# Feature biases of two graph attention layers: from GpSimd to VectorE, and an earlier split of the last residual weights

## The reference, cut to what matters

```
def gat_conv(x, edge_index, W, a_src, a_dst, bias, heads, out_ch, concat):
    xl = (x @ W).reshape(n, heads, out_ch)
    ...
    e = leaky_relu(alpha_src[src] + alpha_dst[dst], 0.2)
    e = exp(e - segment_max(e, dst)[dst])
    alpha = e / (segment_sum(e, dst)[dst] + 1e-16)
    out = segment_sum(xl[src] * alpha[:, :, None], dst)
    return out + bias

h = gat_conv(x, edge_index, W1, a_src1, a_dst1, b1, 4, 256, True)     # 768 -> 4 x 256
h1 = relu(layer_norm(h, g1, be1)) + (x @ Wr1 + br1)
h = gat_conv(h1, edge_index, W2, a_src2, a_dst2, b2, 1, 768, False)   # 1024 -> 768
h = layer_norm(h, g2, be2) + (h1 @ Wr2 + br2)
```

## Time and profile before

| | us |
|---|---|
| median of 3 runs | 1524.95 |
| lowest and highest | 1522.12, 1526.6 |
| span of the profiled execution, first to last instruction | 1524.2 |
| PE busy in it | 1410.7 (93%) |
| DVE busy | 788.4 (52%) |
| POOL busy | 544.3 (36%) |
| ACT busy | 418.4 (27%) |

### The profile page before, as it was taken

The page is one execution under the profiler, slowest core; times in us unless marked ns, Lnnn a source line. Parts: engine busy times, 40 slices in busy tenths (PEclk is TensorE's granted clock), DMA queues, the critical chain, the costliest instruction groups (busy, mean ns, idle before and its releaser), DMA issues.

```text
span 1524.2 us, 22560 instructions
## 1 busy us (share of the span) xinstructions
PE 1410.7 (93%) x7742; PEld 1304.5 (86%) x7742; DVE 788.4 (52%) x1912; ACT 418.4 (27%) x891; POOL 544.3 (36%) x598
## 2 busy tenths in 40 slices
PE   6899799999999999999999899899988999787796
PEld 3667799999999999999999899888878977687783
DVE  7978645233544356563222444544364414599744
ACT  2153511111110011110110311344474324445431
POOL 4000242334233434424424242064324654345530
PEclk9999999999999999999999999899999999967898
DMA  3100111111335233342212121122002211200001
GB/s 110 53 27 6 43 47 37 43 52 49 108 90 154 63 91 102 99 125 63 62 32 63 52 63 32 38 73 84 27 22 73 73 42 37 73 1 1 1 11 51
DMA packets 57652, 86.48 MB, mean 57 GB/s; under 512 B 6442, under 2 KB 54183, under 8 KB 57433
## 3 DMA queue, kind: packets, MB, share of 16 engines
q1 hardware_dynamic: 45184, 66.02, 14.8%
q10 hardware_dynamic: 12374, 19.17, 4.2%
HBM read 83.24 MB, written 1.92 MB: 56 GB/s over the span
## 4 chain that ended last, share of the span: by engine, by line
PE 73%; DVE 14%; POOL 4%; issue 4%; ACT 4%; DMA 1%; DVEq 0%; ACTq 0%; SPq 0%; POOLq 0%
PE psum L2271 13%; PE psum L2274 13%; PE psum L2275 13%; PE psum L2288 8%; PE psum L2291 8%; PE psum L2714 4%; PE psum L2376 3%; DVE max_scratch L1999 2%; PE psum L2764 2%; POOL w_lo L832 2%; PE psum L2615 1%; PE psum L2619 1%; PE psum L2332 1%; PE psum L2620 1%; PE psum L2260 1%
## 5 line engine op out<-in xcount | busy, mean ns | idle before, releaser
L2271 PE MATMUL psum<-w_lo,xT_hi 128*125 128x384 f32 (+5 forms) x1200 | 414.4, 345 | 11.6 <-POOL w_lo L832 4.6
L2274 PE MATMUL psum<-w_hi,xT_lo 128*125 128x384 f32 (+5 forms) x1200 | 408.4, 340 | 0.0
L2275 PE MATMUL psum<-w_hi,xT_hi 128*125 128x384 f32 (+5 forms) x1200 | 408.0, 340 | 0.0
L819 POOL CAST w_hi<-w_raw 128x384 fp32r<-128x384 f32 x190 | 103.2, 543 | 630.9 <-PE psum L2275 492.6
L2271 PEld LDWEIGHTS psum<-w_lo,xT_hi 128*125 128x125 f32 (+1 forms) x1200 | 226.6, 189 | 16.4 <-POOL w_lo L832 7.2
L2274 PEld LDWEIGHTS psum<-w_hi,xT_lo 128*125 128x125 f32 (+1 forms) x1200 | 227.1, 189 | 0.5
L2275 PEld LDWEIGHTS psum<-w_hi,xT_hi 128*125 128x125 f32 (+1 forms) x1200 | 226.6, 189 | 0.0
L1571 DVE TENSOR_TENSOR h_lo<-psum,h_hi 125x384 fp32r<-125x384 f32 (+1 forms) x120 | 66.9, 558 | 301.9 <-ACT h_hi L1018 301.0
L1018 ACT ACTIVATE h_hi<-psum 125x384 fp32r<-125x384 f32 (+1 forms) x120 | 59.1, 492 | 544.7 <-PE psum L2275 540.3
L2288 PE MATMUL psum<-h_lo,adjacency 125*125 125x384 f32 (+3 forms) x600 | 203.6, 339 | 4.6 <-issue 1.9
L821 POOL TENSOR_TENSOR w_lo<-w_raw,w_hi 128x384 fp32r<-128x384 f32 x190 | 201.3, 1060 | 15.2
(11 more groups left out here) (313 smaller groups left out, 2114.9 us busy)
## 6 DMA issues: line engine op xcount, KB each, us to landing
w_raw<-weights_dram SPq DMA_DIRECT2D x296, 192.0 KB, 2.4
score_w_raw<-weights_dram ACTq DMA_DIRECT2D x58, 192.0 KB, 2.8
x_nat<-x_dram SPq DMA_DIRECT2D x1, 1875.0 KB
x_residual<-x_dram SPq DMA_DIRECT2D x1, 1875.0 KB
out_dram<-x_residual SPq DMA_DIRECT2D x5, 375.0 KB
score_a_rows<-L_gnn_a_src_dram ACTq DMA_DIRECT2D x8, 192.0 KB, 3.7
score_a_rows<-L_gnn_a_dst_dram ACTq DMA_DIRECT2D x8, 192.0 KB, 4.7
rgcn_bias<-rgcn_bias_dram SPq DMA_DIRECT2D x1, 1125.0 KB
```

The costliest lines, as they stand in the source:

```text
L819: nc.gpsimd.tensor_copy(mem.wh[:, slot, :], mem.raw[:, raw_slot, :]).then_inc(w_hi_ready, 1)
L2271: ins = nc.tensor.matmul(o, h, wl, start=(j == 0), stop=False, skip_group_check=True)
L2274: nc.tensor.matmul(o, l, wh, start=False, stop=False, skip_group_check=True)
L2275: ins = nc.tensor.matmul(o, h, wh, start=False, stop=stop and j == k - 1, skip_group_check=True)
```

## The change: who adds the feature biases, and when the last residual weights are split

Three things change, all in the order of instructions on GpSimd and VectorE; the arithmetic and its operands stay.

- Q0's five feature biases (three of 125 x 5 x 256 and two of 125 x 5 x 128) go from GpSimd to VectorE: a pair behind the scores of the second head, a pair behind those of the third, the last behind the first three score tiles.
- Q1's five feature biases of 125 x 768 go from GpSimd to VectorE, behind the five products.
- GpSimd, in Q0, splits to chunk 31 instead of 32 behind residual row 4, and to the end of the layer behind row 8 instead of row 9.

```
-            split_to(Q0.chunk + 12)
+            split_to(Q0.chunk + 26)
             pool.wait_ge(params_loaded, 16 * 3)
-            q0_feature_bias(0)
-            split_to(Q0.chunk + 18)
-            q0_feature_bias(1)
-            split_to(Q0.chunk + 26)
-            q0_feature_bias(2)
             for i in range(NB * len(Q0.pieces)):
...
                 q0_residual(i)
                 if i == 4:
-                    split_to(Q0.chunk + 32)
-                elif i == 9:
+                    split_to(Q0.chunk + 31)
+                elif i == 8:
                     split_to(Q0.end)
...
-            split_to(Q1.chunk + 18)
-            pool.wait_ge(b2_loaded, 16)
             split_to(Q1.chunk + 24)
-            for m in range(NB):
-                q1_feature_bias(m)
             pool.wait_ge(params_loaded, 16 * 7)
...
+            def q0_feature_bias(p):
+                dve.wait_ge(gemm_read, Q0.gemm0 + NB * (p + 1))
+                f = mem.feat[0:BP, 0:NB * Q0.heads * Q0.w].rearrange("p (m n) -> p m n", m=NB)
+                for h, u, v, off in features_of(Q0, Q0.pieces[p]):
...
+                    nc.vector.tensor_tensor(t, t, b, ALU.add).then_inc(feat_biased, 1)
+            def q1_feature_bias(m):
+                dve.wait_ge(gemm_read, Q1.gemm0 + NB * len(Q1.pieces))
+                f = feat_flat(Q1, m, 0, D)
+                nc.vector.tensor_tensor(f, f, mem.par[1][0:BP, 0:D], ALU.add).then_inc(feat_biased, 1)
             scores_begin(Q0)
+            dve.wait_ge(params_loaded, 16 * 3)
             for h in range(HEADS2):
                 scores_of(Q0, h)
+                if h in (1, 2):
+                    q0_feature_bias(h - 1)
             for j in range(3):
                 steep_or_flat(Q0, j)
+            q0_feature_bias(2)
             probs(Q0, 2)
...
             for step in (score, finish):
                 for k in range(NB):
                     step(Q1, 0, k)
+            dve.wait_ge(b2_loaded, 16)
+            for m in range(NB):
+                q1_feature_bias(m)
```

More of the change, by code:

```diff
@@ L843, in split_to @@
                 lo_split[0] = max(lo_split[0], end)
-            def q0_feature_bias(p):
-                pool.wait_ge(gemm_read, Q0.gemm0 + NB * (p + 1))
-                f = mem.feat[0:BP, 0:NB * Q0.heads * Q0.w].rearrange("p (m n) -> p m n", m=NB)
-                for h, u, v, off in features_of(Q0, Q0.pieces[p]):
-                    t = f[:, :, h * Q0.w + u:h * Q0.w + v]
-                    b = mem.par[0][0:BP, h * C2 + u:h * C2 + v].rearrange("p (a c) -> p a c", a=1).to_broadcast([BP, NB, v - u])
-                    nc.gpsimd.tensor_tensor(t, t, b, ALU.add).then_inc(feat_biased, 1)
-            def q1_feature_bias(m):
-                pool.wait_ge(gemm_read, Q1.gemm0 + NB * len(Q1.pieces))
-                f = feat_flat(Q1, m, 0, D)
-                nc.gpsimd.tensor_tensor(f, f, mem.par[1][0:BP, 0:D], ALU.add).then_inc(feat_biased, 1)
             def q0_gain(b):
```

2 lines of the change are left out of this document (added).

## The result

The changed kernel takes 1514.74 us in the median of 6 runs (1513.72 to 1519.42), the kernel before 1524.66 in the 6 runs beside them: a ratio of 0.9934, with a 95% interval of 0.9922 to 0.9946. It is 9.9 us faster; forecast were 1514.0 and 10.9.

A forecast was written before the change was run, and what follows sets the result against it. TensorE, busy nearly throughout, was taken as the bound, with only its idle time to win back. 6.4 + 4.5 + 0 = 10.9 us off the 1524.2 us span gave 1513.3, plus 0.75 about 1514.0 us; range 1511.0 to 1518.5.

The forecast's parts named there:

- the first place: Four-head layer: GpSimd splitting ahead of residual row 9 removes TensorE's wait for low halves and the slow clock, 6.4 us.
- The second place: One-head layer: with the five biases off GpSimd, its eight low halves end earlier and TensorE gains 4.5 us.
- five holds of 0.55: One-head layer: each of VectorE's five bias adds delays GpSimd's row adds by 0.55 us, bounds 0 and 0.95.
- The 0.38: One-head layer before the change: a VectorE operation of 0.80 us cost GpSimd 0.38 us (2.19 against 1.81).
- The bound of 5.2: One-head layer, best case: the two engines never meet, ScalarE's high halves set the pace, gain about 5.2 us.
- the forecast's first rival: One-head layer: VectorE's adds hold GpSimd for their whole length, gain 2.5 instead of 4.5 us, 1516.0 us; chance 0.12.
- The start of the four-head layer: Biases moved onto VectorE there: net -0.5 us to about +1.5 us of time, taken as 0.
- that GpSimd is free earlier at this start is worth nothing: Start of the four-head layer: no TensorE wait for low halves stands there, so GpSimd's earlier freedom gains nothing.
- The rival that the start pays: Start of the four-head layer: VectorE's second pair of adds collides, TensorE idles over 2 us, clock falls, 1518.0 us; chance 0.08.
- 0.75 us: Whole kernel: the median of the runs lies 0.75 us above the profiled span, and as much was added to the forecast.
- I let the gain pass to the end: Behind both places engines wait only for TensorE or each other, so the whole 10.9 us reaches the end.

The follow-up runs named there:

- the split alone: The kernel before with only GpSimd's two split edits (to chunk 31 behind residual row 4, to the layer's end behind row 8): 1518.34 us, ratio 0.9963.
- the run with this part alone: The kernel before with only the one-head layer's five feature biases moved from GpSimd to VectorE: 1520.78 us, ratio 0.9976.
- the repeat: The changed kernel measured once more, unaltered, in a later round: 1515.08 us against 1526.06 before, ratio 0.9926.
- the two parts without them: The kernel before with only the two split edits (1518.34 us), and with only the one-head layer's biases on VectorE (1520.78 us).
- the kernel with the additions behind the rows: The changed kernel with VectorE's five one-head-layer bias additions held back until GpSimd's five residual row adds are done: 1514.25 us, ratio 0.9942.
- The earlier rows: The changed kernel with two of the one-head layer's parameter rows loaded earlier, together, with a semaphore of their own: 1517.61 us, ratio 0.9949.

## Why the prediction was right, and where its terms were off

Counted from the mark in front of the four-head layer, the gain of 9.74 us is made up of 6.38 at the first place, 3.73 at the second, 0.3 between them and a loss of 0.66 at the start, where the forecast had 6.4, 4.5 and 0. So the largest term was right in size and in cause, and the two others came out 0.8 and 0.7 us worse.

**The first place held to the digit.** Forecast 6.4, measured 6.38 in the changed kernel, the same tile of 4.84 with the split alone, and 6.2 by its time. GpSimd's five low halves began at 1085.30 and ended at 1090.2 with no wait among them; row 9 and the gain product behind them came in time. The reason held too: put back behind row 9, nine tenths of the gain went.

**The second place is the mis-sized term: 4.5 forecast, 3.7 measured** (3.5 in the run with this part alone and in the repeat). ScalarE's fourth read lies at 1219.00 before and 1211.38 after, 7.62 us apart; with that shift GpSimd's chain reads so in the time of before:

| step | forecast | measured |
|---|---|---|
| sum begins | 1206.0 | 1206.5 |
| eight low halves begin | 1219.6 | 1220.3 |
| they end | 1227.3 | 1228.1 |
| gain | 4.5 | 3.7 |

The steps of the working are right: the start was 0.5 late, as a load still in flight at 1205 to 1206 gives no landing time; the run of six adds was 13.8 us against 13.6; the low halves took 7.85 against 7.72. Three small errors of the same sign make the 0.8. That the six adds came so near was partly luck: the forecast had five holds of 0.55, 2.75 us, and there were in effect four of about 0.7, 2.85. The 0.38 from which the 0.55 was taken divides the 1.9 us by GpSimd's five biases, but only four of VectorE's products stood beside them, which makes it 0.47 for each. The bound of 5.2 was the right one: 5.0 without any meeting of the two engines, and what sets it is ScalarE's high halves, as the prediction said.

**The rule against this part.** The Trainium skill (SBUF — State Buffer, § Who interferes with whom) has the later of the two engines blocked for the other's whole instruction. By that rule, the forecast's first rival, the gain would have been 2.5. With additions of 768 columns the trace shows less, about 0.7 us of 0.95 for each that met, and one of the five hardly met. With 384 columns it shows more than one instruction: 3.9 us in a run of 4.77, over the ends of several.

**The start of the four-head layer**: 0 forecast, 0.7 us of loss measured. VectorE's adds did what was forecast (a pair with both shapes on one row):

```profile
1029.44 2.22 DVE L2082 TENSOR_TENSOR features<-features,par 125x640 f32<-125x640 f32 x2
```

The other pair took 2.22 too, for 2.3, and the last add 1.48 for 1.48: neither pair met a split. But the layer's first reciprocal comes 63.03 us behind the mark, and before 62.36. In the three kernels that leave these biases on GpSimd (before, and the two parts without them) it is 62.2 to 62.4, in all eleven others 63.0 to 63.3. The loss is made ahead of the adds. GpSimd and VectorE before:

```profile
996.57 5.88 POOL L832 TENSOR_TENSOR w_lo<-w_raw,w_hi 128x384 fp32r<-128x384 f32 x6 [30.16 <-ACT w_hi L1160]
1003.19 0.18 DVE L1979 TENSOR_TENSOR al_parts<-al,al_parts 125x20 fp32r<-125x20 f32 x1
```

and after:

```profile
994.97 7.77 POOL L832 TENSOR_TENSOR w_lo<-w_raw,w_hi 128x384 fp32r<-128x384 f32 x8 [29.81 <-ACT w_hi L1136]
1001.85 0.92 DVE L1955 TENSOR_TENSOR al_parts<-al,al_parts 125x20 fp32r<-125x20 f32 x1
```

Without a bias in its list GpSimd goes on to eight low halves, and is still at them when VectorE makes the small operand (`al_parts`) that TensorE waits for. TensorE's wait for it, before and after:

```profile
PE psum L2644 <- DVE al_parts L1979: 2.7, 1, 2.7
PE psum L2642 <- DVE al_parts L1955: 3.7, 1, 3.7
```

In the 9 us that begin 12.8 us behind the mark, in which this wait ends, its granted clock is 0.62 instead of 0.81. VectorE's first search of the layer comes 23.09 us behind the mark instead of 21.01; of these 2.1 us, 1.4 come back by the first reciprocal, most of it where TensorE's waits for score tiles fall from 1.2 us to 0.2. So the step of the working that failed is "that GpSimd is free earlier at this start is worth nothing", with 2.98 us as GpSimd's longest run: the run of 7.77 us cost 2.1. The rival that the start pays came out in sign, but by another wait than the one it names, and with 0.7 us instead of 4. No run leaves only this part out of the changed kernel; by the places it would be about 1 us faster, an estimate from the other two parts' 6.82 + 3.88 = 10.70 us against its 9.74.

**What lies around the span.** I took 0.75 us from the median and one profiled span. In the six runs of the changed kernel the time is 1.7 to 1.8 above the span (1516.58 and 1514.8 in the profiled one), and so it is for runs of the kernel before. The profiled execution of before was thus about 1 us slower than the median. As I took the distance from the median, the two errors cancel: 1514.0 is the median of then less 10.9. Against the gain of 10.9 stand 9.9 us in the medians of the first comparison and 11.0 in the repeat (1526.06 less 1515.08).

**"I let the gain pass to the end"** holds in the median, but not in each execution. Behind the one-head layer's first reciprocal the profiled execution of before has 284.0 us to go, the changed kernel 286.0, its repeat 286.4, the kernel with the additions behind the rows 281.8; over all fourteen it is 281.8 to 287.2. So the changed kernel is 11.35 us ahead there and 9.4 at the end: 1.6 it had ahead of the change, 9.74 are the change's, and 2.0 are lost behind. Of these 2.0, 1.4 lie ahead of the last, eight-head layer (71.90 us from the reciprocal to that layer's first search before, 73.26 after) and 0.6 in it. In that layer TensorE's granted clock differs between two executions of one kernel. The changed kernel and its repeat:

```profile
1330.00:1360.00 30.00, 27.54 (x140) 25.13 (x139) 27.29 (x63) 15.14 (x31) 13.79 (x9) 0.61 0.00 1
...
1330.00:1360.00 30.00, 23.90 (x142) 21.91 (x142) 28.15 (x61) 15.03 (x31) 16.17 (x10) 0.74 0.00 1
```

It is 0.61 in one and 0.74 in the other, beside a VectorE that is busy for 27 to 28 of 30 us in both. But this does not explain the difference, as the two need 286.0 and 286.4 us. What decides it stays open; a gain of an earlier layer passes through here with a spread of several microseconds.

## What to carry to other kernels

Read a gain at its place, between two marks of engines that are not changed themselves (here a reciprocal for each tile, a read before and a reciprocal behind); the total carries the noise of all other stages, and a bare position that of all earlier ones: count it from a mark in front of the edit. When work leaves an engine, ask what else starts that engine, what that then disturbs, and what the new engine's operations cost it while they run side by side, and put the price on the operation that stands beside them at that time, not on the one that was moved. In a list of fixed order, work that another engine is already asking for belongs ahead of anything that may wait, and an earlier transfer is only free if no other engine's transfer needs the queues in those microseconds.

## What the runs showed that was not expected

- VectorE and GpSimd disturbed each other in two ways here. With 768 columns (0.95 us alone) and the 625-column products (0.80 us) they took turns: VectorE's operations grew to 2.0 to 2.6 us and GpSimd's by up to about 0.7. With 384 columns (0.48 us) VectorE's ten ran through, and one GpSimd operation was held for the length of the run, 5.69 and 5.36 us where 1.83 were. Signals between the operations changed neither. Length alone is not a rule: VectorE operations of 5 and 20 columns, 0.18 us alone, were themselves held, to 0.93 to 1.44 us and 0.92. Lengths between 384 and 625 columns were not tried.
- Taking work off GpSimd at the start of the four-head layer cost time, as GpSimd then stood beside an operation of VectorE of 0.18 us that TensorE was waiting for.
- Two loads of 375 KB issued together raised ScalarE's wait for one weight chunk from 2.15 to 6.30 us and TensorE's behind it from 0.99 to 3.84. The earlier rows gave 1.26 us more at the second place (4.99 for 3.73), so more was lost than gained.
